# Moving the rank one-hots of a sort from VectorE to ScalarE in a two-layer graph kernel

## The reference, cut to what matters

```python
def gcn_conv(x, src, dst, ew, W, b):
    deg = segment_sum(ew, dst); dinv = where(deg > 0, rsqrt(deg), 0.0)
    norm = dinv[src] * ew * dinv[dst]
    return segment_sum((x @ W)[src] * norm[:, None], dst) + b
x = layernorm(x + sigmoid(gcn_conv(relu(gcn_conv(x, ..., W1, b1)), ..., W2, b2)))   # with self-loops
z = x @ fc_w.T; rh = edge_attr @ fc_r_w.T
e = leaky(z[src] @ a0 + z[dst] @ a1 + rh @ a2); alpha = softmax of e over each destination's edges
out = layernorm(x + relu(segment_sum(alpha[:, None] * (z[src] + rh), dst) + z @ loop_w))
```

## Time and profile before

| | us |
|---|---|
| time, median of 3 runs | 3388.99 |
| lowest and highest run | 3383.53, 3392.19 |
| span of the profiled execution, first to last instruction | 2442.5 |
| median less that span | 946.5 |
| pass 0, first group sum to first gather of pass 1 | 190 to 827 |

### The profile page before, as it was taken

How to read it: one execution, slowest core, us unless ns; L and a number is a source line. 1 busy time by engine, 2 the same in 40 slices (tenths; PEclk the granted TensorE clock), 3 DMA queues, 4 the chain that set the end, 5 groups by cost and what they waited for, 6 DMA issues and landing times.

```text
span 2442.5 us, 40269 instructions
## 1 busy us (share of the span) xinstructions
PE 1839.8 (75%) x13148; PEld 1626.2 (67%) x13148; DVE 1772.0 (73%) x7010; ACT 1049.6 (43%) x1686; POOL 1770.9 (73%) x1813
## 2 busy tenths in 40 slices
PE   5777668898889687788888783146889788668966
PEld 4656667777778566677777673045778677658866
DVE  7998878888788446676677564178776976586686
ACT  0010012433234135676867666612565268326821
POOL 7777777777775377777777775777777777777771
PEclk9567889999999889899988886567889899879988
DMA  5224222222222423444444433764445555555550
GB/s 142 60 79 134 64 67 74 77 82 78 69 83 64 116 70 100 112 119 126 134 122 118 117 107 92 179 180 134 131 127 150 148 140 132 139 145 134 138 136 20
DMA packets 273634, 270.98 MB, mean 111 GB/s; under 512 B 43718, under 2 KB 218973, under 8 KB 273406
## 3 DMA queue, kind: packets, MB, share of 16 engines
q1 hardware_dynamic: 202366, 142.27, 20.3%
q0 software_dynamic: 57664, 119.62, 19.6%
q10 hardware_dynamic: 13392, 6.46, 0.9%
HBM read 254.63 MB, written 13.96 MB: 110 GB/s over the span
## 4 chain that ended last, share of the span: by engine, by line
POOL 28%; DVE 24%; PE 22%; issue 14%; DMA 7%; ACT 3%; SPq 2%; ACTq 0%; POOLq 0%; DVEq 0%
POOL ring L694 28%; PE ps L829 6%; DVE SR L1535 5%; DVE SR L1572 5%; PE ps L881 5%; DMA ring<-h_d,srcC 2%; PE ps L856 2%; DMA ring<-x_d,srcC 2%; PE ps L869 2%; DMA U<-dlo_d 2%; PE ps L831 2%; DVE U L1612 1%; DVE U L1673 1%; PE ps L843 1%; DVE SR L1645 1%
## 5 line engine op out<-in xcount | busy, mean ns | idle before, releaser
L694 POOL DMA_INDIRECT ring<-x_d,srcC x1132 | 1129.8, 998 | 367.0 <-issue 347.9
L829 PE MATMUL ps<-SR,ring 128*128 128x128 f32 x3604 | 628.9, 308 | 90.8 <-DMA ring<-h_d,srcC 38.1
L694 POOL DMA_INDIRECT ring<-h_d,srcC x526 | 499.7, 950 | 208.1 <-issue 201.7
L829 PEld LDWEIGHTS ps<-SR,ring 128*128 128x128 f32 x3604 | 552.1, 221 | 112.4 <-issue 74.0
L1645 DVE TENSOR_SCALAR SR<-iota_r,cols 128x288 f32<-128x288 f32 x686 | 342.1, 562 | 150.0 <-PE ps L881 150.0
L881 PE MATMUL ps<-SR 128*128 128x288 f32 x1372 | 362.0, 416 | 0.0
L831 PE MATMUL ps<-SR 128*128 128x128 f32 x1564 | 315.0, 296 | 6.0 <-DVE SR L1572 6.0
L881 PEld LDWEIGHTS ps<-SR 128*128 128x128 f32 x1372 | 260.4, 196 | 67.9 <-issue 2.8
L1186 ACT COPY SR<-ps 128x512 f32<-128x512 f32 (+1 forms) x182 | 99.3, 559 | 398.2 <-PE ps L869 398.1
L1572 DVE TENSOR_SCALAR SR<-iota,rankC,ewC 128x128 f32<-128x128 f32 x972 | 264.3, 363 | 1.4 <-DVE U L1776 0.3
L831 PEld LDWEIGHTS ps<-SR 128*128 128x128 f32 x1564 | 258.1, 213 | 6.3 <-issue 6.1
(11 more groups left out here) (286 smaller groups left out, 2578.3 us busy)
## 6 DMA issues: line engine op xcount, KB each, us to landing
SR<-in_edge_attr_dram SPq DMA_DIRECT2D x97, 512.0 KB, 4.3
U<-dlo_d SPq DMA_DIRECT2D x98, 256.0 KB
SR<-low_d SPq DMA_DIRECT2D x84, 256.0 KB
ring<-x_d,srcC POOLq DMA_INDIRECT x1132
ring<-h_d,srcC POOLq DMA_INDIRECT x526
ring<-in_edge_attr_dram SPq DMA_DIRECT2D x12, 512.0 KB
U<-lo_d SPq DMA_DIRECT2D x18, 256.0 KB
ring<-low_d SPq DMA_DIRECT2D x36, 128.0 KB
```

The costliest lines, as they stand in the source:

```text
L694: pool.indirect_dma_start(ring[:, ring_at(p, h if p < 2 else q), k, 0:width], None, (x if p == 0 and h < R0 else table)[:, :], bass.Indire ...
L829: last = nc.tensor.matmul(ps[(p * NA + k) % 2][:, at], ring[:, ring_at(p, h), j, 0:D], S[:, gg % NS, j, :], start=False, stop=stop)
```

## The change

VectorE no longer makes the one-hots of rank. It signals `ranked` once it has the ranks, and goes on to the payload. ScalarE gets a new step `rank_onehot`, after the slot one-hots of the step and before `store_low`: eight activations, one per tile, write the distance |rank - column| into `ohR`, and one activation over all eight tiles (128x1024) turns it into Relu(1 - distance), which is one at the rank and zero elsewhere. It waits for `ranked` and for the block before being `permuted`. TensorE's `permute` waits for it besides `permutable`. Besides, `awT_copied` and `v_made` are merged into `vectors_made`, and `deg_clamped` into `dinv_made`, each with a higher count; the waits on them fall at the same points as before.

```diff
@@ TensorE, permute(s_, g)
                 pe.wait_ge(s("permutable"), n + 1)
+                pe.wait_ge(s("rank_onehot"), 2 * n + 2)
@@ ScalarE
+            def rank_onehot(s_, g):
+                n = s_ * (ST // GT) + g
+                act.wait_ge(s("ranked"), n + 1)
+                if n:
+                    act.wait_ge(s("permuted"), n)
+                for j in range(GT):
+                    last = nc.scalar.activation(ohR[:, j, :], iota[:, :], ACT.Abs, bias=rankF[:, g * GT + j:g * GT + j + 1], scale=-1.0)
+                last.then_inc(s("rank_onehot"), 1)
+                act.wait_ge(s("rank_onehot"), 2 * n + 1)
+                nc.scalar.activation(ohR, ohR, ACT.Relu, bias=ones[:, 0:1], scale=-1.0).then_inc(s("rank_onehot"), 1)
...
                 for m in chunks_at(0, h):
                     slot_onehot(m)
+                for s_, g in made_at(h, 1):
+                    rank_onehot(s_, g)
                 for s_, g in made_at(h, 3):
@@ VectorE, make_ranks(s_, g)
-                link(v.tensor_reduce(ranks, prior, AX.X, ALU.add))
+                v.tensor_reduce(ranks, prior, AX.X, ALU.add).then_inc(s("ranked"), 1)
+                dve.wait_ge(s("ranked"), n + 1)
...
-                for j in range(GT):
-                    v.tensor_scalar(ohR[:, j, :], iota[:, :], ranks[:, j:j + 1], None, ALU.is_equal)
```

More of the change, by code:

```diff
@@ L758, in _ @@
             nc.tensor.transpose(ps[4][:, 3 * P:3 * P + 3], aw3, ident[0:3, 0:3]).then_inc(s("wprod"), 1)
-            pe.wait_ge(s("awT_copied"), 1)
+            pe.wait_ge(s("vectors_made"), 1)
             nc.tensor.matmul(ps[5][:, 0:P], a0B, fcw, start=True, stop=True)
@@ L762, in _ @@
             nc.tensor.matmul(ps[5][:, 2 * P:3 * P], a2B, fcrw, start=True, stop=True).then_inc(s("wprod"), 1)
-            pe.wait_ge(s("v_made"), 1)
+            pe.wait_ge(s("vectors_made"), 2)
             def clear(bank, m):
@@ L1152, in _ @@
                 nc.scalar.copy(deg3[:, k % 2, :], ps[6 + k % 2][0:3, :]).then_inc(s("deg_evac"), 1)
-            act.wait_ge(s("deg_clamped"), 1)
+            act.wait_ge(s("dinv_made"), 1)
             nc.scalar.activation(dtmp[:, 0, :], dtmp[:, 0, :], ACT.Sqrt).then_inc(s("deg_root"), 1)
-            act.wait_ge(s("dinv_made"), 1)
+            act.wait_ge(s("dinv_made"), 2)
             act.wait_ge(s("x_loaded"), 16 * (7 + NSET))
@@ L1501, in weights @@
                 v.tensor_copy(a1B, awT[:, 1:2].broadcast_to([P, P]))
-                v.tensor_copy(a2B, awT[:, 2:3].broadcast_to([P, P])).then_inc(s("awT_copied"), 1)
+                v.tensor_copy(a2B, awT[:, 2:3].broadcast_to([P, P])).then_inc(s("vectors_made"), 1)
                 dve.wait_ge(s("wprod"), 2)
@@ L1505, in weights @@
                 v.tensor_copy(v1B[:, :], ps[5][:, P:2 * P])
-                v.tensor_copy(v2B[:, :], ps[5][:, 2 * P:3 * P]).then_inc(s("v_made"), 1)
+                v.tensor_copy(v2B[:, :], ps[5][:, 2 * P:3 * P]).then_inc(s("vectors_made"), 1)
             def find_odd():
@@ L1543, in _ @@
             link(v.tensor_scalar(dinv[:, :], ps[5][:, 0:NB], 1.0, None, ALU.add))
-            v.tensor_scalar(dtmp[:, 0, :], dinv[:, :], 1e-30, None, ALU.max).then_inc(s("deg_clamped"), 1)
+            v.tensor_scalar(dtmp[:, 0, :], dinv[:, :], 1e-30, None, ALU.max).then_inc(s("dinv_made"), 1)
             link(v.tensor_scalar(dtmp[:, 1, :], dinv[:, :], 0.0, None, ALU.is_gt))
@@ L1548, in _ @@
             v.tensor_tensor(dinv[:, :], dtmp[:, 0, :], dtmp[:, 1, :], ALU.mult).then_inc(s("dinv_made"), 1)
-            dve.wait_ge(s("dinv_made"), 1)
+            dve.wait_ge(s("dinv_made"), 2)
             dve.wait_ge(s("x_loaded"), 16 * (7 + NSET))
```

## The result

| | before | after | ratio, 95% interval |
|---|---|---|---|
| median us, 13 runs each | 3388.45 (3375.34 to 3394.99) | 3406.28 (3390.85 to 3417.27) | 1.0042 [1.0024, 1.0059] |

Slower by 0.4%, some 14 us. The forecast was 3376, its range ended at 3396.

The account below looks back on a forecast made before the run. No engine was full; pass 0's stretch decided, VectorE behind in light steps, TensorE and VectorE in lockstep in loaded ones. -13.5 - 3 - 17 + 9.6 + 13.8 - 2.7 = -12.8 us: 3389 to 3376 us, range 3358 to 3396.

Parts of the forecast that it names:

- the 946.5 us between span and median: Gap between the profiled span of 2442.5 us and the timed median, taken to stay unchanged by the change.
- first gather of pass 1: Sign on GpSimd: if not some 13 us earlier than 826.58 us, the forecast would be wrong.
- Light steps: Pass 0, first nine blocks: VectorE is behind, so its saving passes on, -13.5 us; faster TensorE stretches, -3.
- What is added: ScalarE's 3.60 us block makes TensorE wait after 384 us: eight places, +9.6 us; three set borders, +13.8 us.
- Loaded steps: Pass 0, 384 to 810 us: eleven TensorE waits at the count lose at most 1.57 us each, -17 us.
- clock: -2.7: TensorE in the loaded steps: four or five slow stretches go, two come at steps 56 and 62; -2.7 us.
- waits at L841: Sign: TensorE's waits before the count sum near 35 us instead of 60, none over 4 us.
- the longest waits for the block at steps 56 and 62: Sign: TensorE's longest new waits before the permute come at steps 49, 56 and 62; +3.9 us at 56, +6.2 at 62.
- the 2 us that the prediction had named as a sign of being wrong: Sign: TensorE waits for ScalarE in the light steps longer than 2 us would make the forecast wrong.
- Covered permutes: Rival: ScalarE's block costs nothing at the eight ordinary odd-block places, 9.6 us less; 3367 us, chance 0.15.
- The light steps give little: Rival: TensorE bounds at odd light blocks, four lose 1.05 us each; -3.7 in place of -13.5; 3392 us, chance 0.22.
- ScalarE ends last: Rival: block wholly uncovered at eleven loaded odd blocks and step 49, +46 us against -33.5; 3401 us, chance 0.13.

## Why the prediction was wrong

**The step that failed** is in the sum: "Passes 1 and 2 keep their time, and the 946.5 us between span and median too." It took the difference for something outside the engines' instructions. It lies between them: at the first gather of pass 1 the long execution before is late by 342 us (1167.77 against 825.66), 306 of them at block 8 already. That moved two terms, both against the change:
- *Light steps*, -13.5 and -3 for the clock: -1.1 us by the first pair of traces, +0.1 by the second. VectorE isn't behind there in long executions, it stands still.
- *What is added*, +9.6 and +13.8: 36.8 us at the permute and 4 at the bank's clearing, most of it at step 49. The block is as long as said (3.6 us); it starts later. It lies inside the bounds that were given (0 and 3.6 us a block), and outside what the range was made from.

*Loaded steps*, -17 at the count, held: 17.1. With 17.1 won and 41 lost, TensorE's waits would be up by 24 us; other waits of TensorE there fell (those for the copies of L1186 from 10.0 to 6.0 us, for one). All its waits between blocks 8 and 31 together went from 62.4 to 78.2 us, and the loaded blocks last 15.0 us longer. Less the 1.1 us, that is the +14.0 us at the first gather of pass 1; with the second trace of the changed kernel, from the same group as that of before, it is +16.1. The ratio says +14 us. That these agree so closely is partly chance, as the landmarks are looser than that.

**In the kind of execution that it was read from, the sum was right,** nearly term by term, by one trace each: light blocks -13.3 us (forecast -13.5 and -3), the count -16.7 (-17), the added waits 19.9 + 3.2 = 23.1 (23.4), TensorE's busy time between the blocks -3.2 (clock: -2.7), the first gather of pass 1 earlier by 10.95 us (12.8), waits at L841 30.1 us against "near 35" with one of 4.74 us over the 4, the longest waits for the block at steps 56 and 62 as said, though 3.75 and 7.70 us against 3.9 and 6.2. The whole execution is 15 to 17 us shorter, 11 of them in pass 0; the rest lies in passes 1 and 2, where the sum had nothing, and is within what the kernel before varies by (2436 to 2447 us). In the light steps ScalarE's block held TensorE up by 2.06 us at four places, where VectorE's had held it up by 0.95 before: 4.4 us that the sum lacked, and just over the 2 us that the prediction had named as a sign of being wrong. Against them stand 10.8 us won at the count and 5.0 at waits for VectorE's `S` and bucket one-hots.

**The rivals.** Covered permutes: wrong in both kinds. "The light steps give little", 3392: its result is the long kind's (-1.1 against -3.7), its reason isn't: it needed TensorE to be the bound. Its 1.05 us more at each odd light block did come, in the short kind (1.1), where its result didn't. "ScalarE ends last", 3401, came nearest, with a chance of 0.13. It priced the odd blocks wholly uncovered, at 3.6 us each; 46 with step 62; the waits at the permute came to 36.8 us, some of them (3.86 and 3.38 us) at two even blocks. Its reason, that ScalarE's list is in order and everything behind a late instruction is late, is what the traces show, with the late instruction ahead of the block and not behind it. That its sum fits is partly luck: it kept the light steps' 13.5 us, which didn't come, and had nothing for the other waits that fell.

What argued for doubt was in sight: a profiled span 28% shorter than every timed run. A forecast from such a profile is one for another kind of execution, and its chances have to say so.

## What to carry to other kernels

Compare the profiled execution's own time with the times before costing anything: if they differ by more than a few per cent, a term that rests on "this engine is behind" has to be asked again for the slower kind, where the engine may be idle. Work that moves to another engine's in-order list can inherit the delays of the instructions ahead of it; move only the pieces whose reader comes late (here the light blocks and the even ones behind them: -0.4% in long and -1.6%, by one execution, in short ones, where moving all gives +0.4% and -0.6%). And try the cheap form on the engine it is on first: one wide operation for eight small ones gained 0.7% in short and 0.2 to 0.3% in long executions, with no new wait.

## What the runs showed of the hardware

- One and the same program takes 2441 us in some groups of runs and 3384 to 3422 us in others (medians); within a group the runs of a kernel agree to about 1%. What decides it isn't known. It wasn't the kernel, nor whether it ran once or several times, nor the chip by its number: two short groups and a long one are on record for chip 7, long ones also for chips 4 and 11.
- In the long kind the engines stand still in waits without a releaser in the program (in the trace of the kernel before 270 of over 0.5 us, 2118 us over all engines together: half of them under 3.4 us, six of 50 to 165), while the packets and bytes moved are the same; TensorE's granted clock is then 0.77 on average in place of 0.855. The waits lie at other instructions for each kernel. A kernel can repeat its own closely: in two traces of the changed kernel, from two groups, ScalarE stands still at the four odd light blocks for 7.55, 16.71, 10.28 and 14.67 us, and for 8.29, 16.70, 10.29 and 14.63, and block 31 starts at 1133.7 and 1135.9 us. In a third, from the group in which before took 3422 us, three of the four are 16.9, 18.9 and 5.4 us, the other is absent, and block 31 starts at 1146.6.
- The time of a long execution doesn't grow with the number of ScalarE's instructions (288 more: 0.9999 [0.9983, 1.0015]). Late delivery of instructions would fit the even spacing of TensorE's matmuls at the start, but that is argued and not shown. Whether VectorE's or TensorE's instructions cost by number there wasn't tried apart from their work.
